# Square roots replaced by powers on GpSimd and Newton steps on VectorE, front attention later and a head every 16 slots

## The reference

```python
def _layernorm(x, axis=-1, eps=1e-05):
    m = jnp.mean(x, axis=axis, keepdims=True)
    v = jnp.var(x, axis=axis, keepdims=True)
    return (x - m) / jnp.sqrt(v + eps)
...
qn = q / jnp.maximum(jnp.linalg.norm(q, axis=-1, keepdims=True), 1e-12)
kn = k / jnp.maximum(jnp.linalg.norm(k, axis=-1, keepdims=True), 1e-12)
attn = jnp.einsum('bhld,bhmd->bhlm', qn, kn)
...
attn = jax.nn.softmax(attn + bias[None], axis=-1)
out = jnp.einsum('bhlm,bhmd->bhld', attn, v)
...
h = jnp.concatenate([jnp.broadcast_to(cls_tok, (h.shape[0], 1, h.shape[2])), h], axis=1)
h = h + _L0_attn_ref(_layernorm(h, axis=-1), ...)
h = h + _L0_ffn_ref(_layernorm(h, axis=-1), ...)
```

## Time and profile before

| | |
|---|---|
| median of 3 runs | 3194.76 us (3192.69 to 3196.24) |
| profiled execution | 3193.13 us, span 3191.3 us |
| instructions | 56341 |
| prologue (span's start to first unit) | about 132 us |
| pass 3 (7 images), stages 0 to 7 | 42.36, 45.18, 41.86, 40.20, 40.26, 41.22, 41.50, 36.58 us |
| last pass (5 images, no front), one stage | 28.42 us |
| mean granted clock of TensorE | 0.997 of full speed |

### The profile page before, as it was taken

The page is one execution under the profiler, slowest core; times in us unless marked ns, Lnnn a source line. Parts: engine busy times, 40 slices in busy tenths (PEclk is TensorE's granted clock), DMA queues, the critical chain, the costliest instruction groups (busy, mean ns, idle before and its releaser), DMA issues.

```text
span 3191.3 us, 56341 instructions
## 1 busy us (share of the span) xinstructions
PE 3105.1 (97%) x16588; PEld 2015.8 (63%) x16588; DVE 2428.4 (76%) x8690; ACT 1822.4 (57%) x4758; POOL 1103.7 (35%) x2712
## 2 busy tenths in 40 slices
PE   8989999999999999999999999999999999999998
PEld 8867656655666566555666566556655665676666
DVE  4668778777787778777877787778787877687776
ACT  4555565555555555556555555555556555555555
POOL 2234334432343234333433343334332433333331
PEclk9999999999999999999999999999999999999999
DMA  9111101011001000110001010100111001010110
GB/s 219 34 20 22 22 20 19 19 23 20 19 19 23 20 19 19 21 22 10 19 19 25 19 19 19 25 19 19 19 22 20 19 19 21 18 25 17 26 25 18
DMA packets 92763, 81.25 MB, mean 25 GB/s; under 512 B 56542, under 2 KB 87977, under 8 KB 92457
## 3 DMA queue, kind: packets, MB, share of 16 engines
q1 hardware_dynamic: 91505, 77.26, 12.0%
...
## 4 chain that ended last, share of the span: by engine, by line
PE 77%; DVE 11%; ACT 5%; issue 4%; POOL 3%; ACTq 0%; DMA 0%; POOLq 0%; DVEq 0%
PE ps L687 44%; PE ps L675 15%; DVE wts L1042 5%; ACT wts L858 2%; PE ps L649 2%; PE ps L585 2%; PE ps L700 2%; PE ps L603 2%; PE ps L634 2%; PE ps L716 2%; PE ps L658 2%; DVE top L1026 1%; ACT L858 1%; PE ps L705 1%; PE ps L594 1%
## 5 line engine op out<-in xcount | busy, mean ns | idle before, releaser
L687 PE MATMUL ps<-wts,table 128*128 128x455 f32 (+1 forms) x5120 | 2204.1, 513 | 0.0
L1042 DVE SCALAR_TENSOR_TENSOR wts<-ps,wts 128x455 f32<-128x455 f32 (+1 forms) x2560 | 1459.6, 579 | 594.5 <-ACT wts L858 578.7
L675 PE MATMUL ps<-st,spread 128*128 128x456 f32 (+1 forms) x2560 | 1353.4, 529 | 62.2 <-DVE wts L1042 57.7
L858 ACT ACTIVATE wts<-ps 128x455 f32<-128x455 f32 (+1 forms) x2560 | 1233.2, 513 | 213.5 <-PE ps L675 208.1
L687 PEld LDWEIGHTS ps<-wts,table 128*128 128x128 f32 x5120 | 942.6, 190 | 172.7 <-issue 96.5
L675 PEld LDWEIGHTS ps<-st,spread 128*128 128x128 f32 x2560 | 483.6, 189 | 517.4 <-DVE wts L1042 392.4
L427 POOL TENSOR_TENSOR cand<-best 114x64 f32<-114x64 f32 (+1 forms) x296 | 86.3, 292 | 1033.8 <-DVE best L1010 1033.0
L833 ACT ACTIVATE cand_e<-top,stat 114x16 f32<-114x16 f32 (+1 forms) x296 | 91.2, 308 | 365.9 <-POOL stat L450 364.9
L829 ACT ACTIVATE sc<-ps 114x128 f32<-114x128 f32 (+1 forms) x296 | 82.0, 277 | 370.1 <-PE ps L649 369.9
L443 POOL TENSOR_SCALAR stat<-top 114x1 f32<-114x1 f32 (+1 forms) x296 | 78.5, 265 | 406.8 <-DVE top L1026 402.0
L848 ACT ACTIVATE st<-ps 128x228 fp32r<-128x228 f32 (+1 forms) x296 | 104.8, 354 | 142.6 <-PE ps L658 141.3
(11 more groups left out here) (141 smaller groups left out, 3385.8 us busy)
## 6 DMA issues: line engine op xcount, KB each, us to landing
...
table<-in_table SPq DMA_DIRECT2D x128, 128.0 KB, 6.1
...
rz_dram<-rz SPq DMA_DIRECT2D x56, 1.8 KB
...
```

Of the source, the lines that this page charges most:

```text
L675: mm(ps[0:128, g % NA, 0:t], spread[:, q * 128:(q + 1) * 128], st[:, k % 2, ORDER[c // QUADS], 0:t], start=True, stop=True).then_inc(a_rea ...
L687: mm(ps[0:128, ACC + k % 2, 0:t], table[:, k % H, i, :], wts[:, g % RING, 0:t], start=(c == 0), stop=(c == CH - 1)).then_inc(out_done, 1)
L858: A(wts[:, g % RING, 0:t], ps[0:128, g % NA, 0:t], ACT.Exp).then_inc(e_ready, 1)
L1042: V.scalar_tensor_tensor(out=wts[:, g % RING, 0:t], in0=ps[0:128, g % NA, 0:t], scalar=0.0, in1=wts[:, g % RING, 0:t], op0=ALU.is_ge, op1= ...
```

## The change

Both square roots leave ACT. In the layer normalization ACT only adds eps (`Identity`, whose values need no table of their own), and POOL raises the result to the power -0.5, at the slot where DVE took the reciprocal. For the norms the maximum is taken with 1e-24 of the squared norm on DVE, straight from PSUM, and then 11 DVE instructions on 112 columns (two on the bits as integers, then three rounds of three) give the reciprocal square root. They stand in 11 slots of their own. What follows moves 9 slots back: the spread by POOL from `NRM` + 4 to + 13, the turn from + 6 to + 15, the multiplications from + 7 to + 16, the first task from q = 60 to q = 69. Tasks then follow every 16 slots and no more every 17, so `after_tasks` moves from q = 193 to q = 195 only, and the tasks start at u = 5 and u = 21 of each stage 2 to 5. Before, they started at u = 28, 13, 30, 15, 0, 17, 2 and 19. In the prologue, where the period stays 4, everything from the norms on comes 9 slots later.

```diff
-QK, VAL, NRM, ATT = LN1 + 11, LN1 + 14, LN1 + 17, LN1 + 28
-PERIOD = 17
+QK, VAL, NRM, ATT = LN1 + 11, LN1 + 14, LN1 + 17, LN1 + 37
+PERIOD = 16
...
+            P.memset(power[:, :], -0.5).then_inc(set_pool, 1)
...
+            def layernorm(p, q, n, start):
+                i = 2 * p + n
+                if q == start + 6:
+                    pool.wait_ge(std_ready, i + 1)
+                    P.tensor_tensor(std[:, 0:PASSES[p]], std[:, 0:PASSES[p]], power[:, 0:PASSES[p]], ALU.pow)\
+                        .then_inc(inv_ready, 1)
...
-                    A(std[:, 0:PASSES[p]], ps[0:L, FR, 0:PASSES[p]], ACT.Sqrt, bias=eps[0:L, 0:1])\
+                    A(std[:, 0:PASSES[p]], ps[0:L, FR, 0:PASSES[p]], ACT.Identity, bias=eps[0:L, 0:1])\
...
-                if q == NRM + 1:
-                    act.wait_ge(nrm_mm, p + 1)
-                    A(nrm[:, 0:n * 2 * H], ps[0:L, FR, 0:n * 2 * H], ACT.Sqrt).then_inc(nrm_ready, 1)
...
-                if q == start + 6:
-                    dve.wait_ge(std_ready, i + 1)
-                    V.reciprocal(std[:, 0:PASSES[p]], std[:, 0:PASSES[p]]).then_inc(inv_ready, 1)
...
-                if q == NRM + 3:
-                    dve.wait_ge(nrm_max, p + 1)
-                    V.reciprocal(nrm[:, 0:n * 2 * H], nrm[:, 0:n * 2 * H]).then_inc(nrm_inv, 1)
-                if q == NRM + 7:
+                if q == NRM + 1:
+                    dve.wait_ge(nrm_mm, p + 1)
+                    V.tensor_scalar(nrm[:, 0:n * 2 * H], ps[0:L, FR, 0:n * 2 * H], 1e-24, None, ALU.max)\
                         .then_inc(nrm_max, 1)
+                if 0 <= q - NRM - 2 < NRM_STEPS:
+
+                    step = q - NRM - 2
+                    x, y, t = nrm[:, 0:n * 2 * H], nrm_y[:, 0:n * 2 * H], nrm_t[:, 0:n * 2 * H]
+                    if step == 0:
+                        dve.wait_ge(nrm_max, p + 1)
+                        V.tensor_scalar(t.bitcast(I32), x.bitcast(I32), 1, None, ALU.logical_shift_right)\
+                            .then_inc(nrm_inv, 1)
+                    else:
+                        dve.wait_ge(nrm_inv, NRM_STEPS * p + step)
+                    if step == 1:
+                        V.tensor_scalar(y.bitcast(I32), t.bitcast(I32), -1.0, RSQRT_START, ALU.mult, ALU.add)\
+                            .then_inc(nrm_inv, 1)
+                    if step >= 2 and step % 3 == 2:
+                        V.tensor_tensor(t, y, y, ALU.mult).then_inc(nrm_inv, 1)
+                    if step >= 2 and step % 3 == 0:
+                        V.scalar_tensor_tensor(out=t, in0=t, scalar=-0.5, in1=x, op0=ALU.mult, op1=ALU.mult)\
+                            .then_inc(nrm_inv, 1)
+                    if step >= 2 and step % 3 == 1:
+                        V.scalar_tensor_tensor(out=y, in0=t, scalar=1.5, in1=y, op0=ALU.add, op1=ALU.mult)\
+                            .then_inc(nrm_inv, 1)
+                if q == NRM + 16:
```

More of the change, by code:

```diff
@@ L23 @@
 F32R = mybir.dt.float32r
+I32 = mybir.dt.int32
 ALU = mybir.AluOpType
@@ L61 @@
 EPS = 1e-5
+NRM_STEPS = 2 + 3 * 3
+RSQRT_START = 1597463007.0
 SCALE2 = float(C) ** -0.5
@@ L175, in build @@
         qk_mm, qk_out, qk_sq, v_mm, v_out = sem("qk_mm"), sem("qk_out"), sem("qk_sq"), sem("v_mm"), sem("v_out")
-        nrm_mm, nrm_ready, nrm_max, nrm_inv = sem("nrm_mm"), sem("nrm_ready"), sem("nrm_max"), sem("nrm_inv")
+        nrm_mm, nrm_max, nrm_inv = sem("nrm_mm"), sem("nrm_max"), sem("nrm_inv")
         nrm_spread, nrm_turned, qk_unit = sem("nrm_spread"), sem("nrm_turned"), sem("qk_unit")
@@ L223, in build @@
         eps, mean = sb("eps", [128, 1]), sb("mean", [C, 1])
+        power = sb("power", [L, NMAX])
         h_sb, xh = sb("h_sb", [C, TP]), sb("xh", [128, TP])
@@ L260, in build @@
         hid, rel, mlp1 = (wts[0:META + 1, 0, 0:2 * L - 1], wts[0:3, 1, 0:2 * L - 1], wts[0:3, 2, 0:META])
+        nrm_y, nrm_t = scratch[0:L, 1000:1112], scratch[0:L, 1120:1232]
         kx = sb("kx", [128, 2, TP])
@@ L389, in _ @@
             P.memset(mean[:, :], 1.0 / C).then_inc(set_pool, 1)
-            pool.wait_ge(set_pool, 7)
+            P.memset(power[:, :], -0.5).then_inc(set_pool, 1)
+            pool.wait_ge(set_pool, 8)
             P.memset(w_fold[0:C, :, C:128], 0.0).then_inc(set_pool, 1)
-            pool.wait_ge(set_pool, 8)
+            pool.wait_ge(set_pool, 9)
             P.memset(w_sim[C:128, :, :], 0.0).then_inc(set_pool, 1)
             P.memset(w_fold[C:128, :, 0:C], 0.0).then_inc(set_pool, 1)
-            pool.wait_ge(set_pool, 10)
+            pool.wait_ge(set_pool, 11)
             pool.wait_ge(consts_in, CONSTS)
+            def layernorm(p, q, n, start):
[4 more added lines that the diff above has]
+                        .then_inc(inv_ready, 1)
             def front(p, q):
                 n, t, base = PASSES[p], tokens(p), H * p
-                if q == NRM + 4:
-                    pool.wait_ge(nrm_inv, p + 1)
+                layernorm(p, q, 0, LN1)
+                layernorm(p, q, 1, after_tasks(p) + 6)
+                if q == NRM + 13:
+                    pool.wait_ge(nrm_inv, NRM_STEPS * (p + 1))
                     P.tensor_copy(inv[:, 0:n, :].rearrange("p b (h d) -> p b h d", d=HD),
-                                  by_image(nrm[:, 0:n * 2 * H], n).unsqueeze(3).to_broadcast([L, n, 2 * H, HD]))\
+                                  by_image(nrm_y[:, 0:n * 2 * H], n).unsqueeze(3).to_broadcast([L, n, 2 * H, HD]))\
                         .then_inc(nrm_spread, 1)
@@ L510, in _ @@
             pe.wait_ge(set_act, 5)
-            pe.wait_ge(set_pool, 10)
+            pe.wait_ge(set_pool, 11)
             def layernorm(p, q, n, start):
@@ L572, in front @@
                     last.then_inc(nrm_mm, 1)
-                if q == NRM + 6:
+                if q == NRM + 15:
                     pe.wait_ge(nrm_spread, p + 1)
@@ L906, in _ @@
             dve.wait_ge(set_act, 5)
-            dve.wait_ge(set_pool, 10)
+            dve.wait_ge(set_pool, 11)
             def layernorm(p, q, n, start):
```

3 lines of the change are left out of this document (removed).

## The result

The changed kernel takes 3184.66 us (median of 7 runs, 3181.77 to 3185.45) where the kernel before takes 3195.33 (7 runs on the same chips, 3192.18 to 3196.37). The ratio is 0.9967, 95% interval 0.9955 to 0.9978: 10.7 us faster, about a third of the 29 forecast, and 0.7 us above the range. The profiled execution has a span of 3180.0 us against 3191.3.

A forecast was written before the change was run, and what follows sets the result against it. PE was taken as the bound, waiting about 13 of 329 us per pass of 7. Passes 1 to 6 16.2, pass 7 2.8, pass 0 5.8, pass 8 5.5, prologue -0.9: 29.4 us, so 3165; range 3151 to 3184.

The forecast's parts named there:

- The grid in passes of 5: Stages 2 to 5 of passes 0 and 8: the new task places lose 0.7 and 0.9 us.
- The roots' return in passes of 7: Stages 1 and 6: PE regains 3.5 and 1.7 us per pass once loads and roots leave ACT.
- I leave 0.3 of 3.8: Stage 1 in passes of 7: of 3.8 us of PE waits only 0.3 remain, gain 3.5.
- I leave 0.5 of 2.2: Stage 6 in passes of 7: of 2.2 us of PE waits 0.5 remain, gain 1.7.
- The prologue: Before the first unit: second normalization nearly alone costs 1.6 us (1.0 to 3), less 0.72 returned, net loss 0.9.
- the 0.7 that I gave back for the load: Prologue: with the load at 116.43 gone, PE's 0.72 us wait for ACT's copy goes too.
- The grid in passes of 7: Stages 2 to 5: waits of 6.6 us instead of 4.1, loss 2.5 per pass; stages 3 to 5 near 41.6.
- The power: POOL in the layer normalizations: taken as 0.7 us, between 265 and 1345 ns, costing nothing up to 4.3 us.
- the dear first power: Prologue's first normalization: an uncovered first power of 4 us gives 3169; 1 in 10 of the forecast's chance.
- Newton steps: Eleven DVE steps in stage 1, 0.22 us each (0.15 to 0.30): hidden in passes of 7, some 0.7 showing in passes 0 and 8.
- the grid costs half as much again or more: Rival, stages 2 to 5: 0.4 us more per stage, 14 us lost over 36 stages, time 3179; chance 0.12.
- More comes back: Rival: task stages wait like stage 3 (0.1 us, not 1.5); 40% of the 50 us limit gives 3145; chance 0.08.

The follow-up runs named there:

- the good grid: Changed kernel with the first task at slot 79 from the front of pass 1 on, so tasks at u = 15 and 31: 3144.14 us.
- The short prologue: Kernel with tasks at u = 15 and 31, in pass 0 alone two Newton steps per slot and the first task at slot 62: 3140.45 us.
- the better grid: Kernel before with tasks at u = 15 and 31 from the front of pass 1 on, all roots still on ACT: 3178.79 us.

## Why the prediction was wrong

The direction and the mechanism held, and three terms of the sum were mis-sized: what the grid costs in passes of 5, what the roots give back in passes of 7, and the prologue. Of the 18.6 us between the forecast's 29.4 and the table's sum, 10.3 lie in passes of 7 (pass 7 counted with them), 4.3 in passes 0 and 8, where two misses partly cancel, and 4.0 in the prologue. The grid in passes of 5 and the prologue came out beyond the bounds that the prediction gave them (0.25 us per stage; 1.0 to 3 us).

**The grid in passes of 5** is the largest miss by the stage, 1 us in each of eight: 4.7 and 4.6 us lost against the 0.7 and 0.9 of the step "in passes 0 and 8, where these stages wait already about 3 each, I take 0.7 and 0.9". I took a wait that is there already as room for further work. It is the reverse: PE waits there because DVE is behind, so DVE work that lands where it is behind is paid by PE. (The doubled Newton steps, in slots where it is not, cost 0.3 and 0.03 us in the same two passes.) Pass 0's stages 3 and 4 had taken 32.93 and 31.55 with tasks at u = 15, 0 and 17, while the quiet stage 7, 29.96, had waits of 3.9 in it: the good places had hidden task work of PE (4.4 us a stage) in those waits. The changed kernel's 34.30 has every us of it on top. The grid alone gives the same 34.3, which shows that nothing else in the change does it. My sentence looked at the amount of waiting, not at who waits for whom. Of the 7.7 us that went missing here, 3 were made up by stage 1 of the same passes, which gave 6.5 and 6.8 instead of 5.0 and 5.4.

**The roots' return in passes of 7** was put too high: 2.7 and 1.1 against 3.5 and 1.7, 8.6 us over passes 1 to 6 and most of pass 7's 1.7. The step is "I leave 0.3 of 3.8" and "I leave 0.5 of 2.2". A stage without any front waits 0.9, by my own count, in slots 10 to 23, from the tiles' work on DVE. Stages 1 and 6 have the same tiles and kept waits in slots 9 to 12 and 23; by the same count they now wait about 1.1 each. Had I left the quiet stage's 0.9 in each, the sum would have been 6 us nearer. That is no lower bound, though: the task stages on the good grid wait 0.2 to 0.3, and the stage 3 of the kernel before 0.1. How much a stage keeps depends on where PE's own extra work stands.

**The prologue** lost 4.9 us and not 0.9. Of these 1.2 lie ahead of the token matmul (it starts at 24.95 us before and 26.10 after; over the runs of this study it starts anywhere from 24.95 to 26.75, and in two other kernels with the whole change, period 17 and doubled Newton steps, at 25.64 and 25.46), so most of them can't be laid to the change. The other 3.7 are. I had 1.6 for the second normalization standing alone, in a range up to 3: it is 2.2 of waits, and behind them PE runs at its lower level for a while (granted clock 0.60 over the 4 us from 111 to 115; eight fold matmuls take 1.85 us and not 1.06), 1.2 more by estimate. That part I had not counted at all, and the power that I had put at 0.7 took 1.2 there. It leaves 0.3 of the 3.7 unexplained. The short prologue, in which neither the waits nor the lower clock occur, gives 3.6 back. The grid alone, with the root still on ACT, costs 1.6 there, with 1.2 of waits and a granted clock of 1.00 behind them; the powers alone cost 0.2; the changed kernel costs 3.7: at that place PE turns 0.06 us after the power is done, so its 1.2 us has no cover. And the 0.7 that I gave back for the load did not come: the profile after still has PE waiting 0.73 for the same copy with no load on ACT. The row that I read was true; the cause that I read into it was not. The copy stands in ACT's queue behind an exponential of the first tiles, which waits for POOL. Before, the load filled 1.28 us of that wait and 0.51 was left behind it; now all of it is a wait:

```profile
123.03 0.31 ACT L845 ACTIVATE cand_e<-top,stat 110x16 f32<-110x16 f32 x1 [1.82 <-POOL stat L465]
```

**What held.** The grid in passes of 7: 2.6 lost against 2.5, task stages at 41.6 as written, and stage 2 with waits of 2.1. The split is a little luckier than the total: 1.27 of waits stand by slot 12 where I had 1.5, and the 0.27 in slot 15, which I had called covered, makes up for it. The power: 1.51 us, and from the end of ACT's addition to PE's turn 4.5 to 4.7 us in passes of 7 images and 3.1 to 3.2 in those of 5; it is hidden except in the prologue. That is above the 0.7 taken for it and above its upper bound of 1.345 (a mean over two widths; the 455 columns alone take 1.45), so it was the cover that kept it free, and not the size. The first one took 1.20 us like the others with 5 columns and began 0.18 us after ACT's addition had ended, so the dear first power did not occur. By the Trainium skill (GPSIMD Engine Reference, section "Instruction dispatch") the first call of a freshly loaded kernel pays some 6 us outside the rows; the first turn in the prologue came 10.76 us after the token matmul against 10.84 before, so no run here shows them. Newton steps: 0.25 each, nearly hidden, and 3 us more in all when doubled. The pairs of loads (27 beside the units and not 28 as I had read, since two of the 56 loads stand singly in the prologue) cost PE, net of what replaces them, 38 us on the better grid and, by the run with the grid alone, 57 on the changed kernel's (3242.1 less 3184.7; the changed kernel loses 2 us more in its prologue than that run). What a pair costs depends on its place, from 0.6 to 3.9 us at a normalization, more than on its own 2.85 us of ACT.

**The rivals.** The time fell just outside the range, beside "the grid costs half as much again or more" (3179). That rival's mechanism (0.4 more in each of 36 stages) was not what happened: nothing more in passes of 7, 1 us more per stage in passes of 5. "More comes back" (3145) was turned down because it needs the task stages to wait like stage 3. The run with tasks at u = 15 made them wait nearly like stage 3 (0.2 to 0.3), and took 3144. That both numbers are near 3145 is luck: the rival had its gain beside a full return of the roots and a cheap prologue, and the run had neither.
